# Copying the transposed attention probabilities with ScalarE instead of VectorE, and dropping four weight-cast waits

## The reference

```python
q, k, v = jnp.split(_layernorm(x) @ w_qkv, 3, axis=-1)       # 16 heads of 64, rotary on q and k
scores = jnp.einsum('bhqd,bhkd->bhqk', q, k) / 8
mask = (idx[:, None] >= idx[None, :]) & (idx[:, None] - idx[None, :] < 512)
attn = jax.nn.softmax(jnp.where(mask, scores, finfo.min), axis=-1)
x = x + _layernorm(einsum('bhqk,bhkd->bhqd', attn, v) @ w_out)
y = _layernorm(x); y_prev = y shifted by one token
r = sigmoid((mu_r * y + (1 - mu_r) * y_prev) @ W_r.T)
k_act = square(relu((mu_k * y + (1 - mu_k) * y_prev) @ W_k.T))
out = x + _layernorm(r * (k_act @ W_v.T))
```

## Time and profile before

| what | value |
|---|---|
| median of 2 runs | 2933.59 us (2926.45 and 2940.74) |
| profiled execution | 2922.28 us |
| span of its slowest core (core 7) | 2920.8 us (all cores 2914.9 to 2920.8) |
| TensorE busy | 1247.6 us, 43% of the span |
| VectorE busy | 1044.8 us, 36% |
| ScalarE busy | 475.0 us, 16% |
| DMA | 24 GB/s on average |

### The profile page before, as it was taken

One profiled execution on the slowest core, in us unless ns is written; L12 is line 12 of the kernel. 1 busy time (PEld: TensorE's weight loads), 2 busy tenths in 40 slices (PEclk: granted clock), 3 DMA queues, 4 the chain that ended last, 5 costly groups with the idle time before them and its releaser, 6 DMA issues. The chain is left out here.

```text
span 2920.8 us, 20831 instructions; the slowest of 8 cores (2914.9 to 2920.8 us)
## 1 busy us (share of the span) xinstructions
PE 1247.6 (43%) x7048; PEld 719.9 (25%) x7048; DVE 1044.8 (36%) x1791; ACT 475.0 (16%) x955; POOL 77.4 (3%) x37
## 2 busy tenths in 40 slices
PE   0254443544445454454445444445444043343434
PEld 0132223232232322323223232232322011111111
DVE  2342424333232332322323323232232354646454
ACT  0011111111111211111111111111111012121211
POOL 0000000000000000000000000000000000000000
PEclk9975555555555555555555555555555567676767
DMA  6300000000000000000000000000001501010100
GB/s 190 95 0 8 7 15 1 15 1 15 12 4 15 1 15 15 1 15 1 15 15 1 15 1 15 15 0 15 1 15 35 181 8 51 14 43 22 36 29 22
DMA packets 19813, 70.91 MB, mean 24 GB/s; under 512 B 2944, under 2 KB 2944, under 8 KB 19584
## 3 DMA queue, kind: packets, MB, share of 16 engines
q1 hardware_dynamic: 19712, 69.59, 7.5%
HBM read 52.28 MB, written 17.30 MB: 24 GB/s over the span
## 5 line engine op out<-in xcount | busy, mean ns | idle before, releaser
L544 PE MATMUL PS<-sb_ident,Pb 128*128 128x128 bf16 x1344 | 165.0, 308 | 572.8 <-DVE Pb L524 536.2
L489 ACT ACTIVATE Pb<-PS,sb_consts 128x640 bf16<-128x640 f32 x256 | 224.1, 879 | 879.2 <-DVE PS L465 879.2
L544 PEld LDWEIGHTS PS<-sb_ident,Pb 128*128 128x128 bf16 x1344 | 132.7, 140 | 603.5 <-issue 603.5
L280 PE MATMUL PS<-wqkv_b,xlt 128*128 128x512 bf16 x960 | 250.1, 428 | 23.1 <-DVE xlt L261 23.1
L583 PE MATMUL PS<-PTb,v_ring 128*64 128x128 bf16 x1344 | 167.7, 311 | 177.3 <-DVE PTb L557 177.3
L615 PE MATMUL PS<-wout_b,oT 64*128 64x512 bf16 x544 | 234.8, 629 | 13.2 <-DVE oT L596 13.2
L254 PE MATMUL PS<-sb_ident,xln 128*128 128x128 bf16 x160 | 20.2, 307 | 412.3 <-DVE xln L240 412.3
L583 PEld LDWEIGHTS PS<-PTb,v_ring 128*64 128x64 bf16 x1344 | 139.0, 169 | 209.6 <-issue 209.6
L557 DVE COPY PTb<-PS 128x1280 bf16<-128x1280 bf16 (+1 forms) x136 | 111.1, 817 | 200.4 <-PE PS L544 200.4
L434 PE MATMUL PS<-kT_ring,qTp 128*128 128x128 bf16 x1072 | 145.4, 299 | 29.2 <-DVE kT_ring L386 29.2
L280 PEld LDWEIGHTS PS<-wqkv_b,xlt 128*128 128x128 bf16 x960 | 101.8, 108 | 166.8 <-issue 81.0
(11 more groups left out here) (96 smaller groups left out, 1461.3 us busy)
## 6 DMA issues: line engine op xcount, KB each, us to landing
stag<-wqkv SPq DMA_DIRECT2D x24, 512.0 KB, 4.4
xb<-x_ext SPq DMA_DIRECT2D x20, 512.0 KB, 4.3
x2t<-x2spill SPq DMA_DIRECT2D x20, 512.0 KB, 3.3
x2spill<-x2s SPq DMA_DIRECT2D x17, 512.0 KB, 2.9
out<-outb SPq DMA_DIRECT2D x16, 512.0 KB, 2.6
stag<-wout SPq DMA_DIRECT2D x16, 256.0 KB, 3.5
stag<-wr SPq DMA_DIRECT2D x8, 512.0 KB, 4.6
stag<-wk SPq DMA_DIRECT2D x8, 512.0 KB, 4.7
```

The costliest lines, as they stand in the source:

```text
L280: r = eng.matmul(PSf[:, w * 1024 + half * 512: w * 1024 + half * 512 + 512], lhs, wqkv_b[:, c * 3072 + w * 1024 + half * 512: c * 3072 + w ...
L489: r = eng.activation(Pb[:, poff:poff + 640], PSf[:, hoff:hoff + 640], AF.Exp, bias=CB, scale=CS, accum_out=sums[:, srot + h:srot + h + 1])
L544: r = eng.transpose(PSb[:, pdst + t * 128:pdst + (t + 1) * 128], Pb[:, poff + cc:poff + cc + 128], ident[:])
```

## The change

The copy `ptev` goes from VectorE's `tensor_copy` to ScalarE's `copy`, with the same operands, and its semaphore from `sDVE` to `sACT`. The wait for `ptp` in front of it moves to ScalarE's list, and TensorE waits for `sACT` in place of `sDVE`, both before `av` and before the `sc` two head pairs later. Besides, three waits of TensorE are gone (for `cast` 39 before the first output projection, for `cast2` 15 and `cast2` 23 in the feed-forward part), and two others ask for the last cast at once (`cast` 39 in place of 23 before the first q matmul, `cast2` 23 in place of 7 before the first r matmul).

```diff
                 if j == 0:
-                    S.w("tensor", "sDVE", M[("cast", 23)]["sDVE"])
+                    S.w("tensor", "sDVE", M[("cast", 39)]["sDVE"])
...
-                    for stage, sem in (("exp", "sACT"), ("ptev", "sDVE"), ("nm", "sDVE"),
+                    for stage, sem in (("exp", "sACT"), ("ptev", "sACT"), ("nm", "sDVE"),
                                        ("mk", "sDVE")):
...
-                S.w("vector", "sPE", M[("ptp", qt, hp)]["sPE"])
+                S.w("scalar", "sPE", M[("ptp", qt, hp)]["sPE"])
...
-                        return eng.tensor_copy(PTb[:, prot:prot + ntile * 128], PSb[:, pdst:pdst + ntile * 128])
+                        return eng.copy(PTb[:, prot:prot + ntile * 128], PSb[:, pdst:pdst + ntile * 128])
...
-                M[("ptev", qt, hp)] = S.e("vector", ptev_fn(qt, hp), ("sDVE",), banks={3 * rot, 3 * rot + 1, 3 * rot + 2})
+                M[("ptev", qt, hp)] = S.e("scalar", ptev_fn(qt, hp), ("sACT",), banks={3 * rot, 3 * rot + 1, 3 * rot + 2})
...
-                S.w("tensor", "sDVE", M[("ptev", qt, hp)]["sDVE"])
+                S.w("tensor", "sACT", M[("ptev", qt, hp)]["sACT"])
...
-            if qt == QT0:
-                S.w("tensor", "sDVE", M[("cast", 39)]["sDVE"])
...
-                        S.w("tensor", "sDVE", M[("cast2", 7)]["sDVE"])
+                        S.w("tensor", "sDVE", M[("cast2", 23)]["sDVE"])
...
-                    if ot == 0 and sc == 0:
-                        S.w("tensor", "sDVE", M[("cast2", 15)]["sDVE"])
...
-                    if ot == 0 and sc == 0:
-                        S.w("tensor", "sDVE", M[("cast2", 23)]["sDVE"])
```

## The result

| | kernel before | changed kernel |
|---|---|---|
| median of the runs | 2929.78 us (8 runs) | 2983.19 us (9 runs) |
| profiled execution | 2922.28 us | 2972.02 us |
| span of its slowest core | 2920.8 us | 2970.5 us |

The ratio is 1.0169, 95% interval 1.0149 to 1.0190: slower by 1.7%, 53 us between the medians and 49.7 us between the profiled executions. I had forecast 2989 us and a step of 55.4 us. Of the 5.8 us between 2989 and 2983.19, 3.8 us come from the starting point (the median before is 2929.78 us over 8 runs, where I had 2933.59 over 2), and 2.0 us from the step.

A forecast was written before the change was run, and what follows sets the result against it. It took a single chain through one engine at a time in each head pair as the bound. The dearer copy's 52.7 + 2.7 = 55.4 us, other terms 0, on 2933.6 us gave 2989 us, range 2965 to 3010 us.

The forecast's parts named there:

- What bounds the kernel: Head pairs: a chain with one engine working at a time; TensorE waits for the copy 136 times, 177.3 us in all.
- The copy on ScalarE, 1237 ns: Copy before the v matmuls: 1237 ns against VectorE's 825, priced from ACTIVATE row L292; +55.4 us, bounds -16.2 to +80.0.
- Handovers equal: Engine handovers around the copy: difference taken as 0, with 0.03 us either way, 4 us in all.
- Relief of VectorE buys nothing: VectorE in the head pairs: the 111 us it is relieved of gain nothing, since its next work waits anyway.
- The waits for the casts cost and bring nothing: TensorE's weight-cast waits: later casts asked for delay nothing, three dropped waits save about 0.3 us; taken as 0.
- queued waits: TensorE before the v matmuls: two more waits behind the one that matters, 0.37 against 0.15 us, about 0.11 each.
- Rival A: Wait before the v matmuls: ScalarE's copy or its handover costs more than a plain ACTIVATE; +80 us, 3014 us; chance 0.12.
- Rival B: The copy: ScalarE moves bf16 two at a time, 704 ns a copy, -16 us, 2917 us; chance 0.07.
- Rival C: TensorE's clock: rises with longer pauses, projection at 2.4 GHz saves 117 us; -62 us net, 2872 us; chance 0.03.
- the chances of 0.58 and 0.39: Whole kernel: 0.58 for a time within 2% of the kernel before, 0.39 for slower by over 2%.

The follow-up runs named there:

- experiment 2: Kernel before with only the copy moved to ScalarE, weight-cast waits as before: 2983.0 us, ratio 1.0164.
- experiment 5: Changed kernel with ScalarE copying the same bytes as float32 pairs, 128x640 instead of 128x1280: 2917.8 us, ratio 0.9946 to the kernel before.
- experiment 6: Kernel before with the next head pair's scores, mask and exponential written between this pair's scaling and transposes, copy on VectorE: 2455.5 us, ratio 0.8382.
- experiment 4: Changed kernel with the copy as an ACTIVATE of the Copy function instead of COPY: 2982.0 us, ratio 1.0164 to the kernel before.
- experiment 9: Changed kernel with overlapped head pairs, ScalarE copying before the next exponentials, and the copy as float32 pairs: 2454.3 us, ratio 0.8377 to the kernel before.
- experiment 1: Kernel before with only the weight-cast waits edited as in the change, copy still on VectorE: 2931.2 us against 2932.0, ratio 0.9995.
- experiment 3: Kernel before with TensorE's wait for the copy put last of the three before the v matmuls: 2908.5 us, ratio 0.9918.
- 10: experiment 9 with TensorE's wait for the copy put last of the three before the v matmuls: 2421.1 us, ratio 0.8263 to the kernel before.
- 11: experiment 6 with TensorE's wait for the copy put last of the three before the v matmuls: 2426.7 us, ratio 0.8286 to the kernel before.
- experiment 7: Changed kernel with overlapped head pairs, ScalarE doing the next pair's exponentials before this pair's copy: 2680.2 us, ratio 0.9145 to the kernel before.

## Why the prediction was right, point by point

- *What bounds the kernel: one chain, with the copy on it in all 136 pairs.* Right, and shown from both sides. A longer copy made the kernel slower (experiment 2), a shorter one on the same engine faster (experiment 5), and the reordered pairs took 476 us off with no instruction removed (experiment 6).
- *The copy on ScalarE, 1237 ns.* 1226 measured. The row of L292 carried it, and experiment 4 shows that the difference lies in the choice of instruction. With the measured numbers the term is 128 x (1226 - 825) = 51.3 us and 8 x (1012 - 692) = 2.6 us, 53.9 instead of 55.4. This is the part of the sum that was sized too high.
- *Handovers equal.* Nearly: 0.09 us to ScalarE instead of 0.10, and 0.32 us from its end to TensorE's weight load instead of 0.34. The wait rose by 51.7 us in all, 2.2 less than the copies alone, or 16 ns a time, inside the bound of 0.03 us.
- *The rest.* The spans differ by 49.7 us, 2.0 less than the wait, but that small difference is a balance of larger ones. TensorE is busy 5.2 us longer after (1252.8 against 1247.6), in the q, k, v and the feed-forward matmuls. Its waits for normalised tiles are shorter, from 214.8 to 207.9 us in the feed-forward part (L838, now L836) and from 412.3 to 410.4 at L254. The two traces are of different cores (7 and 5) in different executions, and no run shows that the change causes any of this. So it is partly luck that the 53.4 us between the medians lie within 2.0 us of my 55.4: the wait alone grew by 51.7.
- *Relief of VectorE buys nothing.* Right, also where pairs overlap (experiment 9 against 6: 108 us less work on VectorE, the same time).
- *The waits for the casts cost and bring nothing.* Right (experiment 1). What I said of queued waits, 0.11 us each behind the one that matters, was more useful than its place in the argument: experiments 3, 10 and 11 take 24, 33 and 29 us from it.
- *Rival A* (dearer copy): no, it is cheaper. *Rival B* (two bf16 elements at a time): no. The Trainium skill, "ScalarE: Activation LUTs", section "What ACT_TABLE_LOAD costs", has 0.833 ns per element for fp32 and bf16 alike; experiment 4 agrees, with 1238 - 1025 = 213 ns for 256 columns. The estimate with its fixed part, 1252 ns, is 14 above the measured 1238, and the measurement decides. The Accel of the cycle table in the Trainium skill's "VectorE: DVE Perf Modes" (section on the TRN2 errata) did not show in either instruction; with it as 1 the estimate from the table, 1210 ns, is 16 below the measured 1226. *Rival C* (the clock): the projection took 234.8 us before and 234.7 after, and the granted clock in the pairs is 0.50 in both; no.

The measured 1.69% lies within the 2% to which I gave 0.58. The forecast itself, 1.9%, lay so near that border that the chances of 0.58 and 0.39 for its two sides said little.

## What to carry to other kernels

When no engine is more than half busy, ask which instruction is on the chain and how long it takes there; how much work its engine had in total did not matter here, only what stood directly in front of the copy on it (experiment 7). A bf16 copy of 128x1280 out of PSUM takes 1226 ns on ScalarE and 825 on VectorE, so moving it off the "busier" engine cost 0.4 us each time. And before moving work between the engines of a chain, try to write the next iteration's stages between this one's: here that took 16% off, while moving the bf16 copy made the kernel slower in either order. Where several waits stand in a row, the one that is met last in time should stand last in the list.

## What the runs showed of the hardware

- A wait that was met long ago still costs about 0.11 us of TensorE's time when it stands behind the one that blocks. From the copy's end to the matmul it is 0.37 us with two such waits, 0.26 with one (both in the kernel before) and 0.15 with none (experiment 3).
- On ScalarE, COPY out of PSUM costs 12 to 13 ns less than an ACTIVATE of Copy (1226 against 1238 ns, 1012 against 1025). Both cost 0.83 ns per element, in COPY whatever its size: 1280 bf16 elements take 1226 ns, the same bytes as 640 float32 elements 692 ns (experiment 5). VectorE copies the same 1280 bf16 elements in 825 ns.
- The same 960 q, k, v matmuls took 250.1 us before, 251.6 in the changed kernel and 261.9 in experiment 3, but also 251.0 and 265.6 us on two cores of one execution of experiment 1. A difference of up to 15 us between two traces can come from there alone.
